# A decoder layer on one core: first queries sent in two parts, and splits of weights, x, context, tables and mask moved to other steps of self-attention

## The chip, the cores and the metric

The kernel runs on one core of a Trainium2 chip. The metric is the time of one execution on the device, in microseconds. The kernel before took 874.06 us, the median of three runs (873.6 to 877.2).

## What is computed

One decoder layer with normalisation after each part, on x of 8 batches of 128 tokens of 512 features, in float32:

```
x = layernorm(x + self_attention(x))         # 32 heads of 16, causal, biases
x = layernorm(x + cross_attention(x, ctx))   # 32 query heads, 8 key/value heads of 128, rotary, mask
x = layernorm(x + ffn(x))                    # 4-bit weights, 512 -> 1376 -> 512, silu gate

def self_attention(x):
    q, k, v = x @ Wq.T + bq, x @ Wk.T + bk, x @ Wv.T + bv      # 32 heads
    att = softmax(where(causal, q @ k.T / 4, -inf))
    return (att @ v) @ Wo.T + bo
```

## The kernel before, in words

Each float32 operand is split into a high half and a low half in float16 and each product is done as three float16 products (`split_products`, lines 353 to 355). "High half" is the rounded operand, "low half" what is left of it.

**Self-attention** is done in 8 blocks of 8 steps, with `t` the number of the step, from -12 to 69. A block `j` is one quarter of the heads (8 of them) for one half of x (4 batches). Step `t` of block `j = t // 8`, with `n = t % 8`, has the scores of one batch and four heads. Blocks 0 to 3 use the first half of x, blocks 4 to 7 the second. Every engine runs its own instructions in the order in which the program writes them, step by step, and waits on semaphores; nothing is reordered by the chip. What an engine does in a step beside its regular work is set by tables of step numbers (`W1_SLOT`, `X_SLOT`, `CTX_SLOT`, `TABLE_SLOT`, `MASK_SLOT` and so on).

The regular work of step `t`:

- TensorE (PE): `scores1(t)` (the causal mask as a matmul, line 1579, then two products of stacked keys and queries, line 1582); in steps 4 and 5 of a block a half each of the keys of block j + 2 (`keys1`), in 6 and 7 of its queries (`queries1`), in 0 to 3 a batch each of the values of block j + 1 (`values1`); `weigh1(t - 3)`, the products with the values (lines 1606 to 1608); `turn1(t - 1)`, four transposes of the probabilities (line 1591).
- VectorE (DVE): `row_max1(t)` (line 1114), `p1_lo(t - 2)`, the low half of the turned probabilities, and in even steps `normalise`.
- ScalarE (ACT): `exps1(t)` (lines 764 and 813), `p1_hi(t - 1)`, the high half of the turned probabilities, and in step 6 of a block the keys of block j + 2 out of PSUM (`k1_out_f32`), in step 0 the queries of block j + 1 (`q1_out_f32`).
- GpSimd (POOL): the halves of keys and queries from block 1 on, and of some weights and context.
- SP: all loads, in one queue, among them `stack_rows(j)`: keys and queries of block j go to memory and come back stacked. Step 8j waits for them (`stack_in`).

Beside this, until now:

- ScalarE writes the low and high first queries to memory when both are there (`keep_first_queries`, line 903) and brings them back in three loads (`bring_first_queries`, line 908).
- The third block's weights (`w1_split_hi(2, .)`, `w1_split_lo(2, .)`) get their high halves on ScalarE in steps 0, 1, 2 and their low halves on VectorE one step later. SP issues their load when all stacked rows of block 0 have landed, and the load of the fourth block's weights when these low halves are done. Behind that load stand the second half of the context (`load_ctx(1)`), the rotary tables and `stack_rows(2)`.
- The second half of x gets its four high halves on ScalarE in steps 10, 12, 14, 15, its low halves on VectorE one step later (`x_split_lo(1, k)`). `keys1(4, 0)` of step 20 waits for all of them, and so does SP before `load_ctx(0)`.
- The second half of the context is split on VectorE in steps 9, 11, 25, 29 (`ctx_split`, two instructions each), the tables of the 4-bit weights in steps 18 to 21 (shift, digits, zeros, scales), the mask in step 23.

The part of SP's queue on which much depends:

```
sp.wait_ge(xT_lo, NHALF * NK)      # all eight low halves of x
load_ctx(0)
stack_rows(3)
```

## Time and profile before

| | |
|---|---|
| median of 3 runs | 874.06 us (873.6 to 877.2) |
| profiled execution | 874.4 us, of it 872.5 span |
| granted TensorE clock, mean | 0.998 |
| self-attention, steps 0 to 63 | from 23.45 us on, to about 200 us |

| engine | busy us | share |
|---|---|---|
| TensorE | 831.5 | 95% |
| VectorE | 708.9 | 81% |
| GpSimd | 606.8 | 70% |
| ScalarE | 529.0 | 61% |

Times in the views are microseconds from the start of the span. "Idle before" an instruction is time in which its engine had nothing to do, and the arrow names what ended it. A load is shown where it is issued, on the queue of its engine (SPq, ACTq); how long it took from issue to landing is in a view of its own. Each step of self-attention can be found by its mask matmul, line 1579: step 0 is the first of them.

### The profile page before, as it was taken

How to read it: one execution, taken by the hardware profiler on the slowest of the kernel's cores; microseconds unless marked ns; L12 is line 12 of the kernel's file. 1: busy time of each engine (PE TensorE's matmuls, PEld its weight loads, DVE VectorE, ACT ScalarE, POOL GpSimd, SP SyncE). 2: the span in 40 equal slices, each digit the busy share in tenths (PEclk: the TensorE clock that was granted, in tenths of full speed). 3: DMA queues.
4: the chain of work that ended last, by engine and by line, in shares of the span. 5: the costliest groups of instructions: out<-in, count | busy, mean ns of one | idle time of the engine just before them, and what ended most of it. 6: DMA issues, size and time to landing. Idle time of an engine off the chain costs nothing.

```text
span 872.5 us, 17343 instructions
## 1 busy us (share of the span) xinstructions
PE 831.5 (95%) x6125; PEld 467.0 (54%) x6125; DVE 708.9 (81%) x1098; ACT 529.0 (61%) x1551; POOL 606.8 (70%) x534
## 2 busy tenths in 40 slices
PE   8799999998899999989999999999999989999997
PEld 4577777555445555545555555555555544333344
DVE  5588898987777887799789689698889765899897
ACT  4788888444566665656766665665566752777400
POOL 1165959896656775777776667668888642887895
PEclk9999999999999999999999999999999999999999
DMA  6764245203135413424314214213433213230011
GB/s 178 233 211 166 75 139 167 61 2 121 26 91 140 106 32 83 109 43 157 75 31 127 61 37 122 61 37 86 133 83 46 48 26 89 86 121 14 1 48 49
DMA packets 120037, 76.75 MB, mean 88 GB/s; under 512 B 72877, under 2 KB 104336, under 8 KB 119952
## 3 DMA queue, kind: packets, MB, share of 16 engines
q1 hardware_dynamic: 117504, 74.86, 31.5%
q8 instruction: 49, 0.80, 0.4%
q10 hardware_dynamic: 2448, 0.79, 0.4%
q14 instruction: 36, 0.29, 0.1%
HBM read 52.50 MB, written 6.36 MB: 67 GB/s over the span
## 4 chain that ended last, share of the span: by engine, by line
PE 42%; POOL 22%; DVE 13%; ACT 10%; issue 9%; DMA 3%; SPq 0%; ACTq 0%; DVEq 0%; POOLq 0%
PE bank L353 12%; PE bank L354 12%; PE bank L355 12%; POOL rot L634 4%; POOL q2l L640 3%; ACT prob L964 2%; DVE total L1322 2%; ACT prob L813 2%; POOL pn L651 2%; POOL prob L644 2%; POOL xqs L583 1%; POOL deq L663 1%; POOL left L667 1%; POOL xql L587 1%; DVE rsin L1193 1%
## 5 line engine op out<-in xcount | busy, mean ns | idle before, releaser
L644 POOL TENSOR_TENSOR prob<-prob,rden 128x512 f32<-128x512 f32 x64 | 67.9, 1061 | 116.2 <-DVE rden L1251 116.2
L634 POOL TENSOR_TENSOR rot<-rcos,rsin 128x512 f32<-128x512 f32 x80 | 107.0, 1337 | 18.6 <-DVE rsin L1193 18.6
L353 PE MATMUL bank<-aTh,xqh 128*128 128x512 f16 x256 | 97.1, 379 | 4.1 <-DVE rsin L1193 2.4
L353 PE MATMUL bank<-xoh,o2h 128*128 128x512 f16 x256 | 97.0, 379 | 0.9 <-DVE o2l L1083 0.8
L354 PE MATMUL bank<-xol,o2h 128*128 128x512 f16 x256 | 97.0, 379 | 0.0
L355 PE MATMUL bank<-xoh,o2l 128*128 128x512 f16 x256 | 97.0, 379 | 0.0
L355 PE MATMUL bank<-aTh,xql 128*128 128x512 f16 x256 | 97.0, 379 | 0.0
L354 PE MATMUL bank<-aTl,xqh 128*128 128x512 f16 x256 | 97.0, 379 | 0.0
L964 ACT ACTIVATE prob<-bank,ebias 128x128 f32<-128x128 f32 x256 | 90.6, 366 | 2.1
L1193 DVE SCALAR_TENSOR_TENSOR rsin<-bank,sinq 64x512 f32<-64x512 f32 x128 | 88.0, 688 | 1.7
L651 POOL TENSOR_TENSOR pn<-prob,pn 128x512 f16<-128x512 f32 x64 | 84.0, 1313 | 7.0 <-ACT pn L976 6.8
L640 POOL TENSOR_TENSOR q2l<-rot,q2h 128x512 f16<-128x512 f32 x64 | 82.2, 1284 | 4.4 <-ACT q2h L858 4.4
L858 ACT CAST q2h<-rot 128x512 f16<-128x512 f32 x64 | 39.6, 618 | 74.5 <-POOL rot L634 74.3
L764 ACT ACTIVATE ebias<-nmax 128x4 f32<-128x4 f32 x128 | 26.9, 210 | 78.7 <-DVE nmax L1246 57.6
L813 ACT ACTIVATE prob<-bank,ebias 128x128 f32<-128x128 f32 x256 | 73.2, 369 | 2.1
L976 ACT CAST pn<-prob 128x512 f16<-128x512 f32 x64 | 39.4, 616 | 56.6 <-POOL prob L644 56.4
L1083 DVE SCALAR_TENSOR_TENSOR o2l<-bank,o2h 128x512 f16<-128x512 f32 x64 | 43.4, 679 | 34.7 <-ACT o2h L764 33.9
L1193 DVE SCALAR_TENSOR_TENSOR rcos<-bank,cosq 128x512 f32<-128x512 f32 x64 | 43.7, 683 | 25.6 <-PE bank L355 25.6
L1083 DVE SCALAR_TENSOR_TENSOR pT<-bank,pT 128x512 f16<-128x512 f32 x64 | 43.8, 684 | 13.3 <-ACT pT L764 13.1
L1265 DVE SCALAR_TENSOR_TENSOR res<-bank,res 128x512 f32<-128x512 f32 x64 | 43.8, 685 | 12.3 <-PE bank L355 12.1
L1114 DVE TENSOR_REDUCE nmax<-bank 128x4 f32<-128x512 f32 x64 | 43.7, 683 | 11.3 <-PE bank L1582 11.2
L964 ACT ACTIVATION_READ_ACCUMULATOR prob<-bank,ebias 128x1 f32 x256 | 51.9, 203 | 0.0
(218 smaller groups left out, 2644.2 us busy)
## 6 DMA issues: line engine op xcount, KB each, us to landing
tst<-tables SPq DMA_DIRECT2D x11, 768.0 KB, 5.3
xqs<-in_xwq SPq DMA_DIRECT2D x8, 1024.0 KB, 7.1
xos<-in_xwo SPq DMA_DIRECT2D x8, 1024.0 KB, 5.6
qst<-in_fq SPq DMA_DIRECT2D x11, 384.0 KB, 3.3
kstk<-stack SPq DMA_DIRECT2D x48, 64.0 KB, 2.2
qstk<-stack SPq DMA_DIRECT2D x21, 128.0 KB, 2.5
xs<-in_ctxT SPq DMA_DIRECT2D x2, 1024.0 KB, 7.4
res<-in_x SPq DMA_DIRECT2D x1, 2048.0 KB, 8.3
```

Source lines behind the costliest of these rows:

```text
L353: pe.matmul(out_ap, ah, bh, start=first, stop=False)
L354: pe.matmul(out_ap, ah, bl, start=False, stop=False)
L355: return pe.matmul(out_ap, al, bh, start=False, stop=last)
L634: nc.gpsimd.tensor_tensor(rot[:, r % 2, :], rcos[:, r % 2, :], rsin[:, r % 2, :], ALU.add).then_inc(rope_rot, 1)
L640: nc.gpsimd.tensor_tensor(lo, rot[:, r % 2, :], hi, ALU.subtract).then_inc(rope_lo, 1)
L644: nc.gpsimd.tensor_tensor(prob[:, v % 2, :].rearrange("p (h k) -> p h k", h=QH), prob[:, v % 2, :].rearrange("p (h k) -> p h k", h=QH), rd ...
L651: nc.gpsimd.tensor_tensor(pn[:, v % 2, 1, :], prob[:, v % 2, :], pn[:, v % 2, 0, :], ALU.subtract).then_inc(c_pn_lo, 1)
L813: last = nc.scalar.activation(prob[:, u % 2, j * S:(j + 1) * S], bank[2 + u % 2][:, j * S:(j + 1) * S], ACT.Exp, bias=ebias[:, u % 2, j:j ...
L964: last = nc.scalar.activation(prob[:, v % 2, j * S:(j + 1) * S], bank[2 + v % 2][:, j * S:(j + 1) * S], ACT.Exp, bias=ebias[:, v % 2, j:j ...
L1083: return nc.vector.scalar_tensor_tensor(out=dst, in0=src, scalar=2.0 ** e, in1=hi, op0=ALU.mult, op1=ALU.subtract)
L1193: last = nc.vector.scalar_tensor_tensor(out=as_batches(dst[to, r % 2, :]), in0=as_batches(bank[f % 2][src, :]), scalar=2.0 ** (e - E_X - E_W),
L1265: nc.vector.scalar_tensor_tensor(out=r, in0=bank[6 + v % 2][:, :], scalar=2.0 ** (-E_V2 - E_W), in1=r, op0=ALU.mult, op1=ALU.add).then_inc ...
```

## The change

```
-X_SLOT = {0: 10, 1: 12, 2: 14, 3: 15}
-CTX_SLOT = {(1, 0): 9, (1, 1): 11, (1, 2): 25, (1, 3): 29}
+X_SLOT = {0: 10, 1: 13, 2: 15, 3: 17}
+X_LO_SLOT = {0: 11, 1: 15, 2: 17, 3: 19}
+CTX_SLOT = {(1, 0): 9, (1, 1): 23, (1, 2): 25, (1, 3): 33}
...
-TABLE_SLOT, MASK_SLOT, BIAS_SLOT, SCALES_SLOT = 18, 23, 17, 26
+TABLE_SLOTS = 26, 27, 30, 31
+MASK_SLOT, BIAS_SLOT, SCALES_SLOT = 34, 17, 26
...
-                sp.wait_ge(q1_out, 32 * (j + 1))
+                sp.wait_ge(q1_out, 32 * j + 16)
...
+            stack_rows(4)
             sp.wait_ge(tab_ready, 2)
             for t, src in enumerate((z1, sw)):
                 sp.dma_start(tables_d[t], src[:, :]).then_inc(tab_out, 16)
-            stack_rows(4)
             stack_rows(5)
...
-                pool.wait_ge(q1_out, 32 * j)
+                pool.wait_ge(q1_out, 32 * j - 16)
+                if j == 1:
+                    pool.wait_ge(q1_first, 16)
...
-            def keep_first_queries():
+            def keep_first_high():
+                act.wait_ge(first_hi, 2)
+                act.dma_start(stack_d[0, 2], q1h[:, :]).then_inc(q1_first, 16)
+
+            def keep_first_low():
                 act.wait_ge(first_lo, 2)
-                for i, src in enumerate((q1h, q1l)):
-                    act.dma_start(stack_d[0, 2 + i], src[:, :]).then_inc(q1_out, 16)
+                act.dma_start(stack_d[0, 3], q1l[:, :]).then_inc(q1_out, 16)

             def bring_first_queries():
-                act.wait_ge(q1_out, 32)
                 for slot, part in enumerate((2, 2, 3)):
+                    if part == 2:
+                        act.wait_ge(q1_first, 16)
+                    else:
+                        act.wait_ge(q1_out, 16)
...
+                if t == FIRST + 4:
+                    keep_first_high()
                 if t == FIRST + 5:
-                    keep_first_queries()
+                    keep_first_low()
...
-                if t in (0, 1, 2):
-                    w1_split_hi(2, t)
+                if t in (2, 3, 4):
+                    w1_split_hi(2, t - 2)
...
-                if t in (1, 2, 3):
-                    w1_split_lo(2, t - 1)
-                for k, slot in X_SLOT.items():
-                    if slot == t - 1:
+                if t in (3, 4, 5):
+                    w1_split_lo(2, t - 3)
+                for k, slot in X_LO_SLOT.items():
+                    if slot == t:
...
-                    if t == TABLE_SLOT + step:
+                    if t == TABLE_SLOTS[step]:
...
+                if t == 0:
+                    values1(1, 0)
                 if 0 <= t < STEPS1:
                     scores1(t)
...
-                if j + 1 < BLOCKS and n < 4:
+                if j + 1 < BLOCKS and n < 4 and t != 0:
                     values1(j + 1, n)
```

The high first queries are written as soon as they are there, the low ones when they are, and the two loads that need only the high ones are issued without waiting for the low ones. The third block's weights are rounded in steps 2, 3, 4 (low halves 3, 4, 5). The high halves of the second half of x go to steps 10, 13, 15, 17, the low ones to 11, 15, 17, 19. Two pieces of context move from step 11 to 23 and from 29 to 33, the tables from 18 to 21 to 26, 27, 30, 31, the mask from 23 to 34, and SP writes the tables behind block 4's rows. On TensorE the first value product of block 1 moves ahead of the first scores.

On TensorE at step 0, before (the scores are the first two rows, lines 1579 and 1582; `[waits ...]` are semaphores):

```order
L1579 MATMUL bank<-tri,identb 128x512 [waits consts_ready,stack_in0]
L1582 MATMUL bank<-kstk,qstk 128x256 x2
L353 MATMUL bank<-w1h,aTh 128x128 [waits k1_f32,w1_lo]
L354 MATMUL bank<-w1l,aTh 128x128
L355 MATMUL bank<-w1h,aTl 128x128
```

and in the change, from the last three of the twelve value matmuls on:

```order
L355 MATMUL bank<-w1h,aTh 128x128
L356 MATMUL bank<-w1l,aTh 128x128
L357 MATMUL bank<-w1h,aTl 128x128
L1591 MATMUL bank<-tri,identb 128x512 [waits consts_ready,stack_in0]
L1594 MATMUL bank<-kstk,qstk 128x256 x2
```

The twelve value matmuls now stand ahead of the wait for the stacked rows (`stack_in0`), not behind it.

On VectorE in steps 18 to 20, before, from the normalising of step 18 on (`znb` are the table digits, `nmax` the row maxima, `pT` the low half of the probabilities):

```order
L1270 TENSOR_TENSOR znb<-tz,shz 33x512 [waits codes_tab_in]
L1114 TENSOR_REDUCE nmax<-bank 128x4 [waits exp_done,s_psum]
L1083 SCALAR_TENSOR_TENSOR pT<-bank,pT 128x512 [waits pv_done,pT_hi]
L1280 TENSOR_SCALAR znb<-znb 33x512 [waits tab_step]
L1114 TENSOR_REDUCE nmax<-bank 128x4 [waits exp_done,s_psum]
```

and in the change:

```order
L1142 TENSOR_TENSOR onrm<-bank,rden 128x128 [waits rden_done]
L1126 TENSOR_REDUCE nmax<-bank 128x4 [waits exp_done,s_psum]
L1095 SCALAR_TENSOR_TENSOR pT<-bank,pT 128x512 [waits pv_done,pT_hi]
L1095 SCALAR_TENSOR_TENSOR aTl<-xs,aTh 128x512 [waits xT_hi]
L1126 TENSOR_REDUCE nmax<-bank 128x4 [waits exp_done,s_psum]
```

The table shift and digits are gone from here, and x's last low half (`aTl`) stands in the place of the digits.

## Rows read from the trace of the kernel before

**Rows 1.** TensorE's waits, 0 to 345 us: total us, times, longest

```profile
PE bank L1591 <- ACT prob L813: 7.8, 8, 2.6
```

**Rows 2.** Timeline, TensorE, opening: start us, us, what [idle before <-releaser]

```profile
23.45 0.39 PE L1579 MATMUL bank<-tri,identb 128*128 128x512 bf16 x1 [1.66 <-DMA qstk<-stack]
...
24.56 0.38 PE L1579 MATMUL bank<-tri,identb 128*128 128x512 bf16 x1
...
30.63 0.66 PE L1591 MATMUL bank<-ident,prob 128*128 128x128 f32 x4 [2.62 <-ACT prob L813]
```

**Rows 3.** Timeline, ScalarE and its queue, opening

```profile
16.36 0.45 ACTq L906 DMA_DIRECT2D stack<-q1l  x1
...
19.43 1.99 ACTq L911 DMA_DIRECT2D qstk<-stack  x3
...
28.68 0.63 ACT L764 ACTIVATE w1h<-w1s 128x512 f16<-128x512 f32 x1 [1.90 <-DMA w1s<-in_wvT]
```

**Rows 4.** DMA issues up to 60 us: KB each, us from issue to landing

```profile
xs<-in_ctxT SPq DMA_DIRECT2D x1, 1024.0 KB, 9.1
...
stack<-q1l ACTq DMA_DIRECT2D x1, 128.0 KB, 3.1
```

**Rows 5.** Timeline, TensorE: steps 8, 19, 24, 32, 40, 48 and two stalls

```profile
43.92 0.38 PE L1579 MATMUL bank<-tri,identb 128*128 128x512 bf16 x1
...
57.97 0.17 PE L1606 MATMUL bank<-v1h,pT 128*128 128x17 f16 x1 [1.44 <-DVE onrm L1130]
...
71.19 0.38 PE L1579 MATMUL bank<-tri,identb 128*128 128x512 bf16 x1
...
83.87 0.38 PE L1579 MATMUL bank<-tri,identb 128*128 128x512 bf16 x1
...
103.41 0.38 PE L1579 MATMUL bank<-tri,identb 128*128 128x512 bf16 x1
...
122.12 0.38 PE L1579 MATMUL bank<-tri,identb 128*128 128x512 bf16 x1
...
129.81 0.17 PE L1606 MATMUL bank<-v1h,pT 128*128 128x17 f16 x1 [0.54 <-DVE onrm L1130]
...
140.88 0.38 PE L1579 MATMUL bank<-tri,identb 128*128 128x512 bf16 x1
```

**Rows 6.** Timeline, SP's queue: third block's weights, and context behind the fourth's

```profile
23.41 0.40 SPq L392 DMA_DIRECT2D w1s<-in_wkT  x1
...
36.91 0.52 SPq L479 DMA_DIRECT2D xs<-in_ctxT  x1
```

**Rows 7.** Timeline, VectorE: context (step 11), x's last low half, shift, digits

```profile
53.19 1.38 DVE L1093 TENSOR_SCALAR cTh<-xs 128x512 f16<-128x512 f32 x1
54.61 0.98 DVE L1083 SCALAR_TENSOR_TENSOR cTl<-xs,cTh 128x512 f16<-128x512 f32 x1
...
67.50 0.68 DVE L1083 SCALAR_TENSOR_TENSOR aTl<-xs,aTh 128x512 f16<-128x512 f32 x1
...
72.11 0.85 DVE L1270 TENSOR_TENSOR znb<-tz,shz 33x512 int32<-33x512 int32 x1
...
74.08 1.51 DVE L1280 TENSOR_SCALAR znb<-znb 33x512 int32<-33x512 int32 x1
```

**Rows 8.** Timeline, SP's queue: context, and the query loads of block 3

```profile
68.21 0.38 SPq L479 DMA_DIRECT2D xs<-in_ctxT  x1
...
77.40 1.37 SPq L425 DMA_DIRECT2D qstk<-stack  x3
```

**Rows 9.** DMA issues, 78.3 to 78.6 us: the last of those three

```profile
qstk<-stack SPq DMA_DIRECT2D x1, 128.0 KB, 4.0
```

**Rows 10.** Stretches: us, busy of PE, PEld, DVE, ACT, POOL, clock, DMA, GB/s

```profile
28.00:30.00 2.00, 0.01 (x1) 0.00 (x0) 0.66 (x2) 1.29 (x5) 0.69 (x1) 1.00 0.47 158
...
238.00:240.00 2.00, 2.00 (x16) 1.90 (x15) 1.75 (x4) 1.51 (x3) 2.00 (x3) 0.50 0.02 4
```

**Rows 11.** Timeline, TensorE, the stall ahead of the lower clock

```profile
236.97 0.91 PE L1658 MATMUL bank<-ident,res 128*128 128x128 f32 x4 [2.98 <-DVE rsin L1193]
```

More of the change, by code:

```diff
@@ L318, in decoder_kernel @@
         qk_hi, qk_lo = sem("qk_hi"), sem("qk_lo")
-        k1_out, q1_out, stack_in = sem("k1_out"), sem("q1_out"), [sem("stack_in0"), sem("stack_in1")]
+        k1_out, q1_out, q1_first, stack_in = sem("k1_out"), sem("q1_out"), sem("q1_first"), [sem("stack_in0"), sem("stack_in1")]
         s_psum, nmax_done, ebias_done, exp_done = sem("s_psum"), sem("nmax_done"), sem("ebias_done"), sem("exp_done")
```

## Prediction, before the changed kernel was run

> **What bounds the kernel now.** I read the page first: TensorE is busy for 95% of the span, so there are some 40 us in all to be won, and only where TensorE waits. The whole change lies in the first 48 steps of self-attention. The list of TensorE's waits up to 345 us comes next; its longest entry is the transposes of the probabilities, 7.8 us in 8 times [rows 1]. The timeline then tells where. At step 0 TensorE stands 1.66 us until the first queries have landed; at step 1 it stands 2.62 us, because ScalarE has not written the second probabilities [rows 2]. ScalarE in its turn was held for 1.90 us by the third block's value weights, still on their way [rows 3]. At 57.97 there is a third stall, 1.44 us, behind VectorE [rows 5]. The rest of the stretch is nearly tight: the eight steps from 122.12 to 140.88 take 18.76 us with one stall of 0.54 in them, so an unhindered block of eight takes about 18.2 [rows 5]. A reader should keep two questions apart: how early a step could start, and whether its stacked keys and queries have landed by then.
>
> **Opening, part by part.** The low first queries are issued at 16.36 and land 3.1 us later [rows 3, 4]; only then are the three loads issued, from 19.43 for 1.99 us [rows 3]. In the change the high ones are written about 1 us earlier, two of the three loads go ahead of the low ones' landing, and the third is issued at some 19.1 instead of 21.0. So the queries land near 21.7, when TensorE ends its work anyway (23.45 less the idle 1.66 is 21.8). The first value product of block 1 now stands ahead of the first scores: 12 matmuls, step 0's 1.11 us less 0.44 for the scores [rows 2], 0.67. Scores of step 0 at 22.5 instead of 23.45.
>
> The third block's weights now leave ScalarE after three exponentials instead of before the second. The load is issued at 23.41, when the queries have landed [rows 6], and was awaited until 28.68 [rows 3]; issued near 21.9 it is in by 27.2, and ScalarE comes to it at 29.3. The transposes of step 1 follow 2.8 us after step 0's scores and one exponential later, at 27.1 instead of 30.63. Some comes back: the key product of step 4 wants the low half of these weights, which VectorE can end only at 30.9, 0.85 us after TensorE gets there. From step 5 on ScalarE has the same work as before. Step 8, at 43.92 before [rows 5], then starts at 40.6: **-3.3** (between -2.0, if only the DMA wait of 1.9 goes, and -3.8 without the key wait).
>
> **Steps 9 to 14.** What was moved later lets step 9 down: its piece of context stays where it was. The context is issued at 36.91 and lands 9.1 us later, 46.0 [rows 4, 6]. It is queued behind the fourth block's weights, which wait for the third block's last low half, now two steps later. I put its issue at 38.6 and its landing at 46.0 again, since less is in flight ahead of it. VectorE gets there at 44.7 and stands 1.4 us; step 12 has won only 1.9. At step 11 the second piece of context goes away, 1.38 and 0.98 us [rows 7], and with it the stall of 1.44. Step 14 began right behind those products, at 58.7, and now starts at 55.3: **-3.4** (between -2.5 and -5.0 without the wait for the context).
>
> **The step on which it turns: 19.** x's last low half moves from 67.50 [rows 7] in step 16 to the place where the digits now stand, 74.08 [rows 7]. The table shift of 0.85 ahead of it is gone and ScalarE has one high half less before it; in the time base of before it ends at 73.5. Less the 3.4 won that is 70.1, where it was 68.2. Two engines wait for it. TensorE's key product of step 20 needs it: 1.0 us of idle. And SP: the load of the first half of the context waits for all of x and sits **ahead of block 3's stacked rows** on the same queue. In the trace the context is issued at 68.21, right behind x's last half; the last three query loads of block 3 start at 77.40 for 1.37 us and the last of them, at 78.35, needs 4.0 us [rows 8, 9]. That is 14.2 us from x to stacked queries, and nothing of the 14.2 is changed. Before they lay there at 82.35 and step 24 began at 83.87 [rows 5]: 1.5 us of slack. Now they are there at 70.1 + 14.2 = 84.3, while TensorE would be ready at about 80.0. It stands 4.3 us at step 24, and all that was won before is gone: **+0.4** at step 24 (between -1.2 and +1.3, from the bounds of step 14).
>
> **Blocks 3 and 4** (83.87 to 103.41 to 122.12 [rows 5]; 19.54 and 18.71 us, 1.3 and 0.5 above 18.2). Block 3 loses the context piece of step 29 and gains shift and digits, 0.85 and 1.51 us [rows 7], behind the piece of step 25; walking VectorE, ScalarE and TensorE through the eight steps I get 19.1, **-0.4**. Block 4 takes the piece at step 33 and the mask at step 34, of about 0.7 us; TensorE stands some 0.6 at step 35, where before it stood 0.4 at step 32: **+0.2** (each within 1 us). The fifth block's rows no longer wait behind the tables; they had a slack of many microseconds. The tables now wait for step 31, ahead of block 5's rows, which GpSimd ends only after step 30's keys: nothing. The mask and the tables are wanted from step 62 on: nothing, covered by 20 steps and more. GpSimd's new wait for the high queries is long met. The piece of context in step 23 lies under the stall of step 24; if that cover is gone it costs what it cost at step 11, up to 1.4.
>
> **Sum:** 874.4 (the profiled execution, span 872.5 and 1.9 around it) + 0.4 - 0.4 + 0.2 = 874.6; the median of the runs is 0.3 lower, so **874.2**. From the bounds its own range is 872.4 to 876.4.
>
> **The clock.** Around 28 to 30 TensorE did next to nothing for 2 us, in a stall of 2.62, and the granted clock stayed at 1.00. Before 236.97 it did nothing for 2.98 us, and from 238 to 240 the granted clock is 0.50, the lower of the two levels, 1.2 GHz [rows 2, 10, 11]. A stall of 4.3 us at step 24 is longer than either. Two to three and a half microseconds of tight work at half the clock would cost 1.0 to 1.7 us. The Trainium skill (TensorE: Matmul & The Clock Gate, section "The HAM clock gate") says that the gate cuts the clock to half after TensorE has been idle and gives it back only after it has been busy for a while. By that rule this change, which gathers several small stalls into one long one, is worse than its idle time tells; the trace agrees at 238 and does not at 28.
>
> **Rivals.**
> 1. *No stall at step 24.* If the loads of block 3 get through faster than 14.2 us (the last load alone took 4.0, where first queries took 3.1 [rows 4, 9]), or x is finished earlier, the 3.4 us of step 14 and about 0.6 of block 2 stay: 874.2 - 3.4 - 0.6 - 0.2 = 870.0. Against it: it needs the whole 4.3 us, and the order on SP's queue is the same in both kernels. Half of it gives 872.
> 2. *The clock falls at step 24*, by the paragraph above: 874.2 + 1.2 = 875.4.
> 3. *Slower: VectorE falls behind in steps 25 to 27.* Piece, shift and digits in three steps running are at their longest 1.38 + 0.98 + 0.85 + 1.51 = 4.7 us on top of 1.4 a step, against 2.0 us a step of TensorE. It is 3.0 late then, less the 0.9 that the chain allows; I had 0.9 in the sum. It decides if GpSimd's work runs beside all four, since I take these lengths for its doing (a low half of the same shape takes 0.68 or 0.98 [rows 7]). Once in block 3 and once, with the mask, in block 4: 874.2 + 1.2 + 1.0 = 876.4, more where the context also lands late.
> 4. *The change doesn't do what it says in the opening*: ScalarE's write of the high queries lands no earlier, since it shares the way with six key loads. Step 0 is then unchanged and the later steps still win 2; since step 24 hangs on the other end, the total is hardly touched: 874.6.
>
> **How the numbers follow.** What a measurement of this kernel can tell from no change is about 0.5%, 4.4 us. The forecast (rival 4 in it) has 0.50, rival 1 or half of it 0.22, rival 2 0.18, rival 3 0.10. Below 869.7 lies about half of rival 1 with the wait for the context also gone, 0.13; above 878.4 only rivals 2 and 3 together with a late context, 0.05; between them 0.82. The range leaves out a tenth at either end: 869.6 to 877.0.
>
> **What would show it.** In the profile after: the first scores near 22.5 and no wait of ScalarE for weights; a wait of VectorE for the context before step 9's piece; x's last low half near 70; SP issuing the context right behind it and the queries of block 3 some 9 to 10 us later; TensorE idle for 3 to 5 us before the scores of step 24, put down to the stacked queries; and step 40 near 122 as before. If step 24 starts before 82 without such an idle, the argument on SP's queue is wrong and the kernel is faster; if the granted clock shows 0.50 near 84, rival 2 is at work.

## The result, and the profile after

The changed kernel takes **878.45 us** (median of 8 runs, 874.4 to 880.37) where the kernel before takes 874.34 beside it (8 runs, 873.59 to 877.2). The ratio is 1.0037, 95% interval 1.0026 to 1.0049. Measured a second time, it took 880.04 beside 874.38, ratio 1.0055 (1.0041 to 1.0069). So the change makes the kernel slower, by about half a per cent; the forecast was 874.2 with a range up to 877.0, and the measured time lies 1.4 us above that range. The profiled execution took 878.48 us, of it 876.6 span, 4.1 more than the span of before.

The list of TensorE's waits up to 345 us; the columns are who waited for whom, then us in total, times, longest:

```profile
PE bank L1603 <- ACT prob L817: 4.8, 4, 1.6
PE bank L1618 <- DVE onrm L1142: 4.0, 4, 2.0
PE bank L1591 <- DMA qstk<-stack: 3.6, 2, 3.0
```

The longest entry of before, the wait for the probabilities, has fallen from 7.8 us in 8 times [rows 1] to 4.8 in 4. In its place stand a wait for VectorE's normalised product of 2.0 us and one for stacked queries of 3.0. The timeline of TensorE in the change says where (mask matmuls, L1591, mark the starts of steps 0, 8, 12, 14, 24, 32, 40, 48 and 63):

```profile
22.66 0.39 PE L1591 MATMUL bank<-tri,identb 128*128 128x512 bf16 x1 [0.56 <-DMA qstk<-stack]
...
25.46 0.66 PE L1603 MATMUL bank<-ident,prob 128*128 128x128 f32 x4 [1.08 <-ACT prob L817]
...
30.88 0.39 PE L355 MATMUL bank<-aTh,w1h 128*128 128x512 f16 x1 [0.59 <-DVE w1l L1095]
...
40.60 0.38 PE L1591 MATMUL bank<-tri,identb 128*128 128x512 bf16 x1
...
49.75 0.17 PE L1618 MATMUL bank<-v1h,pT 128*128 128x17 f16 x1 [2.00 <-DVE onrm L1142]
...
50.80 0.63 PE L1591 MATMUL bank<-tri,identb 128*128 128x512 bf16 x1
...
57.34 0.38 PE L1591 MATMUL bank<-tri,identb 128*128 128x512 bf16 x1
...
71.83 0.38 PE L355 MATMUL bank<-aTh,w1h 128*128 128x512 f16 x1 [0.86 <-issue]
...
84.81 0.61 PE L1591 MATMUL bank<-tri,identb 128*128 128x512 bf16 x1 [3.00 <-DMA qstk<-stack]
...
104.98 0.38 PE L1591 MATMUL bank<-tri,identb 128*128 128x512 bf16 x1
...
124.28 0.38 PE L1591 MATMUL bank<-tri,identb 128*128 128x512 bf16 x1
...
143.42 0.38 PE L1591 MATMUL bank<-tri,identb 128*128 128x512 bf16 x1
...
197.41 0.38 PE L1591 MATMUL bank<-tri,identb 128*128 128x512 bf16 x1
...
248.01 0.43 PE L355 MATMUL bank<-aTh,xqh 128*128 128x512 f16 x1 [2.13 <-DVE aTl L1095]
```

The rows of before that answer to 57.34, 197.41 and 248.01 and were not shown yet (timeline of TensorE, kernel before: steps 14 and 63, and the same product of cross-attention):

```profile
58.74 0.38 PE L1579 MATMUL bank<-tri,identb 128*128 128x512 bf16 x1
...
194.89 0.38 PE L1579 MATMUL bank<-tri,identb 128*128 128x512 bf16 x1
...
245.51 0.38 PE L353 MATMUL bank<-aTh,xqh 128*128 128x512 f16 x1 [0.78 <-DVE aTl L1083]
```

From these rows and [rows 5], after less before, and what the prediction said of each:

| | before | after | difference | forecast |
|---|---|---|---|---|
| step 8 | 43.92 | 40.60 | -3.32 | -3.3 |
| step 14 | 58.74 | 57.34 | -1.40 | -3.4 |
| step 24 | 83.87 | 84.81 | +0.94 | +0.4 |
| step 32 | 103.41 | 104.98 | +1.57 | 0.0 |
| step 40 | 122.12 | 124.28 | +2.16 | +0.2 |
| step 48 | 140.88 | 143.42 | +2.54 | +0.2 |
| step 63 | 194.89 | 197.41 | +2.52 | +0.2 |
| end of the span | 872.5 | 876.6 | +4.1 | +0.2 |

The gain of the opening is there to two hundredths of a microsecond. It is lost in three places: between steps 8 and 14, at step 24 with what follows it, and once more between 197 and 252 us, in a part of the kernel that the change does not touch. Another 1.0 us goes between steps 32 and 48, in two smaller pieces. The clock shows at each of the first three. Stretches of the change, with the columns of [rows 10] (the third number from the right is the granted clock):

```profile
50.00:52.00 2.00, 2.00 (x16) 1.32 (x13) 1.60 (x4) 1.97 (x7) 1.85 (x3) 0.56 0.58 176
52.00:54.00 2.00, 2.00 (x9) 0.75 (x8) 1.32 (x3) 1.97 (x7) 2.00 (x2) 0.59 0.52 142
...
84.00:86.00 2.00, 1.19 (x7) 0.79 (x8) 0.11 (x1) 0.00 (x0) 1.31 (x2) 0.59 0.77 180
86.00:88.00 2.00, 2.00 (x28) 2.00 (x27) 1.66 (x4) 1.35 (x5) 0.00 (x0) 0.56 1.03 392
...
248.00:250.00 2.00, 1.99 (x6) 0.78 (x7) 1.66 (x3) 0.87 (x5) 0.77 (x1) 0.55 0.01 1
250.00:252.00 2.00, 2.00 (x7) 0.74 (x6) 0.00 (x0) 1.97 (x9) 0.00 (x0) 0.60 1.01 165
```

Behind each of the stalls of 2.00, 3.00 and 2.13 us TensorE runs for about four microseconds at a mean clock of 0.55 to 0.60, that is mostly at 1.2 GHz. The mask matmul of 0.63 at 50.80, where it takes 0.38 elsewhere, is the same thing seen in one instruction.

What released the first two stalls is on VectorE and on SP's queue. VectorE's timeline of the change, step 9's piece of context, step 10's normalised product and x's last low half:

```profile
46.42 0.53 DVE L1105 TENSOR_SCALAR cTh<-xs 128x512 f16<-128x512 f32 x1 [1.86 <-DMA xs<-in_ctxT]
...
49.31 0.29 DVE L1142 TENSOR_TENSOR onrm<-bank,rden 128x128 f32<-128x128 f32 x1
...
70.94 0.78 DVE L1095 SCALAR_TENSOR_TENSOR aTl<-xs,aTh 128x512 f16<-128x512 f32 x1
```

SP's queue in the change, the two loads of context and the query loads of block 3:

```profile
38.51 0.51 SPq L481 DMA_DIRECT2D xs<-in_ctxT  x1
...
71.75 0.38 SPq L481 DMA_DIRECT2D xs<-in_ctxT  x1
...
81.34 1.37 SPq L427 DMA_DIRECT2D qstk<-stack  x3
```

VectorE stands 1.86 us for the context at step 9. SP issues the next context when x's last low half ends at 71.7 (70.94 + 0.78). Behind it on the same queue stand the writes of block 3's keys and queries to memory (issued from 72.26 on) and the loads that bring them back stacked (from 78.13 on); the query loads come 9.6 us after x, and TensorE starts step 24 at 84.81, 13.1 us after x: the chain of the prediction, link by link.

### The profile page after: what moved, and what is told of

It is laid out like the page before. It is cut to its first block, busy times and chain, and to the rows that moved or that the text cites. A ratio compares the mean times of both kernels' runs of the same rounds, so it can differ in the third digit from the quotient of the medians.

```text
span 876.6 us, 17343 instructions
## 1 busy us (share of the span) xinstructions
PE 834.1 (95%) x6125; PEld 467.6 (53%) x6125; DVE 710.2 (81%) x1098; ACT 530.2 (60%) x1551; POOL 607.5 (69%) x534
## 4 chain that ended last, share of the span: by engine, by line
PE 43%; POOL 23%; DVE 12%; issue 9%; ACT 8%; DMA 4%; SPq 1%; DVEq 0%; POOLq 0%; ACTq 0%
PE bank L355 12%; PE bank L356 12%; PE bank L357 12%; POOL rot L638 4%; POOL q2l L644 3%; POOL pn L655 2%; DVE total L1334 2%; ACT prob L976 2%; POOL prob L648 2%; POOL left L671 1%; POOL xqs L587 1%; POOL deq L667 1%; ACT prob L817 1%; POOL xql L591 1%; DVE rsin L1205 1%
## 5 line engine op out<-in xcount | busy, mean ns | idle before, releaser
L988 ACT CAST pn<-prob 128x512 f16<-128x512 f32 x64 | 39.4, 615 | 57.2 <-POOL prob L648 56.9
```

## Experiments

Each kernel was timed in five rounds beside the kernel before on the same chip. That took 874.92 us beside x_early, opening, ctx_behind and busy, 874.85 beside x_alone and the three with the first piece of context late (these four ran on another chip than the rest), 874.89 beside x_alone_behind, all_three and busy_q, and 874.38 beside the last. All edits are to the changed kernel unless it says otherwise, and each kernel has a label, by which the expectations and tables name it.

### x back in its early steps (x_early), and the opening alone (opening)

```
-X_SLOT = {0: 10, 1: 13, 2: 15, 3: 17}
-X_LO_SLOT = {0: 11, 1: 15, 2: 17, 3: 19}
+X_SLOT = {0: 10, 1: 12, 2: 14, 3: 15}
+X_LO_SLOT = {0: 11, 1: 13, 2: 15, 3: 16}
```

> The changed kernel with the second half of x split in the steps of before (high halves 10, 12, 14, 15, low halves one step later); all the rest as changed. Theory A (queue): x's last low half ends near 64, SP issues the context and block 3's rows then, and they have landed by about 78, so TensorE has no stall before step 24 and no half clock behind it. Step 24 starts near 81 and the kernel takes 872 to 873, 1 to 2 us below before. Theory B (VectorE is overfull in blocks 3 and 4 through tables, context and mask): step 24 moves but the blocks behind it stay long, and the kernel stays at 876 or above. The stall of 2 us in step 11 and the half clock behind it are there under both.

**871.95 us** (870.88 to 874.37), ratio 0.9966 (0.995 to 0.9982). No stall at step 24, which begins at 82.07, 1.1 us later than theory A had it.

The second kernel has that edit too, and context, tables, mask and SP's order as in the kernel before, so that only the opening is changed:

```
-CTX_SLOT = {(1, 0): 9, (1, 1): 23, (1, 2): 25, (1, 3): 33}
-TABLE_SLOTS = 26, 27, 30, 31
-MASK_SLOT, BIAS_SLOT, SCALES_SLOT = 34, 17, 26
+CTX_SLOT = {(1, 0): 9, (1, 1): 11, (1, 2): 25, (1, 3): 29}
+TABLE_SLOTS = 18, 19, 20, 21
+MASK_SLOT, BIAS_SLOT, SCALES_SLOT = 23, 17, 26
```

> Only the opening of the change: first queries written apart, first value product ahead of the first scores, third block's weights two steps later; x, context, tables and mask in the steps of before, SP's order as before. Theory A: step 8 starts near 40.6 (3.3 us earlier); VectorE then waits 1.9 us for the context in step 9 and has the second piece in step 11, so a part is given back; no stall before step 24. Kernel 871.5 to 873.5. If the opening itself were harmful, because what follows waits for loads in any case, it would take 874 or more.

**872.72 us** (871.75 to 874.67), ratio 0.9976 (0.9965 to 0.9986). The opening alone is worth 2.2 us, and moving the second piece of context, the tables and the mask costs nothing in sum (871.95 with them, 872.72 without, and the intervals overlap). The loss of the change comes in with the slots of x.

### The slots of x alone in the kernel before (x_alone), and with SP's queue turned round (x_alone_behind)

The kernel before with the slots of x of the change:

```
-X_SLOT = {0: 10, 1: 12, 2: 14, 3: 15}
+X_SLOT = {0: 10, 1: 13, 2: 15, 3: 17}
+X_LO_SLOT = {0: 11, 1: 15, 2: 17, 3: 19}
...
-                    if slot == t - 1:
+                    if slot == t:
```

> The kernel before with one edit: the high halves of the second half of x in steps 10, 13, 15, 17 and the low ones in 11, 15, 17, 19, everything else (opening, context, tables, mask, queue order) as before. Theory A (x's last low half holds the context's load, which holds block 3's stacked rows): step 20 lies near 73, x's last low half ends near 74.5, and the queries of block 3 land 13.1 us later as in the change, at 87.6; TensorE stands about 3 us or more ahead of the scores of step 24, which begin at 87 to 88 instead of 83.87; with the clock halved behind that stall 878 to 880.5. Rival B (the slots of x cost nothing themselves, the change loses by VectorE's and ScalarE's new pieces in later steps): step 24 within 1 us of 83.9, 874 to 875.5.

**879.65 us** (877.45 to 881.5), ratio 1.005 (1.0036 to 1.0063). TensorE at step 24 and SP's queue ahead of it:

```profile
88.44 0.61 PE L1580 MATMUL bank<-tri,identb 128*128 128x512 bf16 x1 [2.31 <-DMA qstk<-stack]
```

```profile
74.53 0.38 SPq L480 DMA_DIRECT2D xs<-in_ctxT  x1
...
85.03 1.39 SPq L426 DMA_DIRECT2D qstk<-stack  x3
```

The context is issued at 74.53, right behind x's last low half; the query loads at 85.03; step 24 starts at 88.44 instead of 83.87. Then the same kernel with two entries of SP's queue turned round:

```
-            sp.wait_ge(xT_lo, NHALF * NK)
-            load_ctx(0)
             stack_rows(3)
+            sp.wait_ge(xT_lo, NHALF * NK)
+            load_ctx(0)
```

> The kernel before with the x slots of the change, as in x_alone (879.65 us, step 24 at 88.44), and the queue turned round: SP loads block 3's stacked rows ahead of the first half of the context. Theory A (the loss of x_alone goes through SP's queue): no stall behind the stacked queries, step 24 at 84.5 to 85.5, only the key product of step 20 waits 1.4 us for x's last low half; no half clock near 84 to 88; 875 to 876.5. Rival B (the x slots cost VectorE or TensorE time by themselves): step 24 at 87 or later, 878 or more.

**874.61 us** (873.33 to 877.03), ratio 1.0002 (0.9991 to 1.0013), 0.4 below the range of theory A. SP's queue and step 24 now:

```profile
73.95 1.37 SPq L426 DMA_DIRECT2D qstk<-stack  x3
75.37 0.43 SPq L480 DMA_DIRECT2D xs<-in_ctxT  x1
```

```profile
84.92 0.38 PE L1580 MATMUL bank<-tri,identb 128*128 128x512 bf16 x1
```

x's last low half ends at 73.47, in x_alone at 74.50 (all of this difference stood already at step 8, 43.24 for 44.27). The query loads come 11 us earlier, there is no wait for them, and 5.0 us of the kernel's time are back. This pair shows the cause: the slots of x cost through the wait for x that stands ahead of block 3's stacked rows. With the queue turned, step 24 still begins 1.05 us later than in the kernel before (TensorE's wait of 1.44 us for x at the key product of step 20, with the half clock behind it), but block 3 takes 18.34 us instead of 19.54, and in sum nothing is left. Whether the turn of the queue alone would make the kernel before faster was not run.

### The same turn of the queue in the change (ctx_behind)

> The changed kernel with one thing turned round on SP's queue: block 3's stacked rows first, then the wait for all of x and the first half of the context. x stays late. Theory A: the key product of step 20 still waits 0.9 us for x, but the stall of 3.0 us before step 24 and the half clock behind it go: step 24 near 82, kernel 872.5 to 874. If instead the late x itself (VectorE, step 20) were the cause, step 24 would stay near 84 to 85 and the kernel at 877 to 878.

**873.74 us** (871.62 to 874.92), ratio 0.9984 (0.9973 to 0.9994), 4.7 below the change, as theory A had it. Step 24 starts without a wait, 1 us earlier than expected:

```profile
81.01 0.38 PE L1591 MATMUL bank<-tri,identb 128*128 128x512 bf16 x1
```

### TensorE kept busy in the two stalls (busy), by matmuls whose results nobody reads

```
+                if t == 24:
+                    pe.wait_ge(exp_done, 23)
+                    for _ in range(12):
+                        pe_.matmul(bank[2][:, :]..., identb[:, :], tri[:, :]..., start=True, stop=True)
...
+                if t == 11:
+                    pe.wait_ge(q1_f32, 3)
+                    for _ in range(8):
+                        pe_.matmul(bank[1][:, :]..., identb[:, :], tri[:, :]..., start=True, stop=True)
```

> The changed kernel with matmuls that compute nothing wanted put into two stalls of TensorE: 8 in step 11 (1.7 us of the 2.0) and 12 before step 24 (2.6 us of the 3.0), into banks that are free there. The waits stay; only the idle time is filled. Clock theory: the granted clock stays at 1.00 around 50 to 54 and 84 to 88, the work behind each stall takes its full-clock time, 1.5 us less behind step 11 and 1.3 us less behind step 24: kernel 875.5 to 876.5. Rival (the half clock costs nothing because other engines bound those steps anyway): 878 to 878.5, as changed.

**875.43 us** (874.44 to 880.01), ratio 1.001 (0.9996 to 1.0024): twenty matmuls more, and the kernel is 3.0 us faster than the change. The stretches behind the two stalls:

```profile
50.00:52.00 2.00, 1.44 (x21) 1.19 (x21) 1.67 (x6) 1.97 (x8) 1.85 (x3) 1.00 0.28 87
52.00:54.00 2.00, 2.00 (x24) 1.34 (x22) 1.28 (x3) 2.00 (x7) 2.00 (x2) 1.00 0.48 141
84.00:86.00 2.00, 1.53 (x21) 1.07 (x20) 0.57 (x1) 0.00 (x0) 1.24 (x2) 1.00 0.80 201
86.00:88.00 2.00, 2.00 (x38) 1.84 (x36) 1.70 (x5) 1.81 (x7) 0.00 (x0) 1.00 1.02 376
```

What released the stalls comes no earlier (step 24 begins at 84.79, in the change at 84.81), but the clock behind them is 1.00. Steps 8 to 14 take 15.59 us (41.20 to 56.79) instead of 16.74, and steps 24 to 32 take 18.90 (84.79 to 103.69) instead of 20.17: the half clock cost 1.15 and 1.27 us where it fell. (Counted from the end of the wait at step 11 to step 14, the change takes 7.59 us and busy 6.16. The change profiled again, below, takes 6.16 as well: its clock stayed at 1.00 there with no matmul added. So the half clock itself costs 1.43 at the first place; in busy 0.28 of it is lost again because the wait ends that much later after step 8.) The first of the two does not reach step 24, which hangs on the queries. The second does reach the end, less what another half clock near 164 us takes back: step 63 begins 1.15 earlier than in the change (196.26). The other 1.35 of the 2.5 between the two profiled spans (874.1 and 876.6) lie behind step 63, of which more below.

### The first piece of context in a later step (ctx0_late), with the turned queue, with the early x, and with both

```
-CTX_SLOT = {(1, 0): 9, (1, 1): 23, (1, 2): 25, (1, 3): 33}
+CTX_SLOT = {(1, 0): 21, (1, 1): 23, (1, 2): 25, (1, 3): 33}
```

> The change with one edit: the first piece of context is split in step 21 instead of 9, so that VectorE waits for no load at step 9; x and the queue order as in the change. Theory A: VectorE's wait of 1.9 us at step 9, TensorE's stall of 2.0 at step 11 and the half clock behind it go; step 14 begins at 54.5 to 55.5 instead of 57.34, and x's last low half ends near 69 to 70; step 24 still stands behind the stacked queries, 13.1 us after x, at 82.5 to 83.5 instead of 84.81, with a stall of 3 us or more and the half clock behind it. So 876 to 877.5: about two thirds of what is won at step 14 comes through. Rival B (step 24 is not bound by x): the whole gain of 2 to 3 us at step 14 and no stall at 24, 872 to 874.

**874.03 us** (872.83 to 876.59), ratio 0.9993 (0.9984 to 1.0001). Step 14 begins at 53.95 and step 24 at 82.12, behind a stall of 3.35 us, both a little earlier than theory A had them. The median fell by 4.4 us, more than A's 1 to 2.5, and lies at the edge of rival B's 872 to 874, so the time does not decide between them. The profile does: the stall at step 24 is there, as only A has it, but A priced the piece too low. The profiled execution took 875.54, 2.9 less than that of the change, and 2.7 of it is there at step 24. From step 8 to step 14 this kernel takes 12.90 us (41.05 to 53.95) and the change 16.74; the 3.84 between them are TensorE's stall of 2.00 and 1.84 of half clock and what follows from it. This is the step where the prediction's 3.4 went.

With SP's queue turned round as well (ctx0_late_behind):

> The change with two edits: the first piece of context is split in step 21 instead of 9, and SP loads block 3's stacked rows ahead of the first half of the context. Theory A: neither the stall at step 11 nor the one at step 24 is left, step 14 near 55, step 24 at 79.5 to 80.5, and no half clock up to 230 us; what is left is block 3's own work. 870.5 to 873. Rival B (VectorE, which now has context pieces in steps 21, 23 and 25 and the shift and digits in 26 and 27, is the next to bind): step 24 as said, but step 32 more than 19.8 us later than it, 873 to 875.

**869.52 us** (869.1 to 869.86), ratio 0.9936 (0.9924 to 0.9948), the lowest median of all, though the intervals of the next two kernels overlap with it. It is 1 us below the range of theory A. Step 24 starts at

```profile
77.97 0.38 PE L1591 MATMUL bank<-tri,identb 128*128 128x512 bf16 x1
```

without a wait, 5.9 us before that of the kernel before and 1.5 earlier than expected, and the granted clock is 1.00 up to 230 us. Step 32 follows at 97.73, 19.76 behind; rival B's bound of 19.8 was not passed.

With x in its early steps instead of the turned queue (ctx0_late_x_early):

> The change with two edits: the first piece of context is split in step 21 instead of 9, and the halves of x are back in steps 10, 12, 14, 15 and 11, 13, 15, 16. Theory A: the opening's 3.3 us come through to step 14 (near 55.5) and to step 24 (80 to 81), since x's last low half ends at 65 to 66 and the queries land before 80. With x_early at 871.95 and its stall of 2.69 at step 12 with the half clock behind it gone, 869.5 to 871.5. Rival B (something later takes the gain back): within 0.5 of x_early.

**870.01 us** (869.88 to 870.15), ratio 0.9942 (0.9929 to 0.9955). The time is in the range of theory A; step 14 at 53.08 and step 24 at 77.59 both lie 2.4 us earlier than it had them. And with all three edits (all_three):

> The change with three edits: first piece of context in step 21, block 3's stacked rows ahead of the context on SP's queue, x back in steps 10, 12, 14, 15. Theory A: of ctx0_late_behind (869.52) the key product's wait of 1.26 us at step 20 goes, step 24 begins at 77.0 to 77.6, 868.5 to 869.5. Rival B: blocks 3 and 4 are bound by VectorE behind it, and step 32 stays at 97.7: within 0.3 of 869.7.

**869.74 us** (869.2 to 871.73), ratio 0.9947 (0.9934 to 0.996). The time is rival B's: the key product no longer waits and step 24 comes 0.31 earlier (77.66), but step 32 lies at 97.86, no earlier than with two edits. That VectorE binds block 3 there is not shown: TensorE waits for it 0.6 us in the block, in the kernel with two edits as well. Either way of freeing the queries is enough, and they do not add.

### The rest of the loss, behind 197 us

In the change the last 1.6 us are lost where nothing was changed. The stall of 2.98 us is at 236.97 before [rows 11] and at 239.50 after. Before, the clock fell behind it (0.50 from 238 to 240, [rows 10]) and the next stall, at 245.51, was 0.78. After, it stayed at 1.00, the next stall, at 248.01, was 2.13, and the clock fell there. From the one stall to the other both took the same (8.54 and 8.51 us): VectorE sets that time, TensorE only waits more or works more slowly. Behind the second stall TensorE no longer waits for VectorE, and there the half clock costs its full price: the nine products from 248.01 on take 3.62 us, those from 245.51 on 1.94. From the mask matmul of step 63 to the end of the span:

| half clock behind the | kernel: us |
|---|---|
| first stall | before 677.6, x_early 677.1, opening 677.3, busy 677.8, x_alone_behind 677.2, ctx0_late_behind 677.7, ctx0_late_x_early 678.1, all_three 678.1 |
| first, twice as long | x_alone 678.2 |
| second stall | change 679.2, change again 678.7, ctx_behind 679.3, ctx0_late 678.9 |

(The labels are those of the expectations above; "before" and "change" are the two kernels.) These sums still mix the place of the half clock with what comes later. A fixed instruction shortly behind the second stall parts the two; it is VectorE's fifth reciprocal of cross-attention, here before and in the change:

```profile
250.42 0.18 DVE L1251 RECIPROCAL rden<-dens 128x4 f32<-128x4 f32 x1
```

```profile
254.61 0.18 DVE L1263 RECIPROCAL rden<-dens 128x4 f32<-128x4 f32 x1
```

It comes 55.5 us after the mask matmul of step 63 before, and 57.2 in the change, so the whole 1.6 us is lost by then. In the nine kernels whose half clock falls behind the first stall it comes after 55.5 to 55.9 us, in the four profiles of the last row after 57.2 each time: the place costs 1.3 to 1.7 us. From there to the end all fourteen profiles (busy_q, below, included) take 621.5 to 622.5 us. The four highest of these, x_alone, ctx0_late_x_early, all_three and busy_q, are those with one more stretch of half clock between 388 and 404 us.

One kernel was to test this, busy_q, with eight more matmuls, read by nobody, in the second stall of the change:

```
+                    if what == (2, 0):
+                        for _ in range(8):
+                            pe_.matmul(dst[:, :]..., identb[:, :], tri[:, :]..., start=True, stop=True)
                     pe.wait_ge(fill_free, find_fill("t", 0, BH * ORDER[n][1] + BH - 1) + 1)
```

> The change with eight matmuls more, 1.7 us of TensorE work whose result nobody reads, in the stall of 2.13 us ahead of the query product of the third block of cross-attention (248.01 in the change). Everything up to 245 us as in the change. Theory A (the last 1.65 us of the loss is the clock at half behind this stall, in the place where it was not in the profile before): the granted clock is 1.00 from 248 to 252, the nine products of 0.43 us take 0.22, and the kernel takes 876.5 to 877.3. Rival B (the loss there is the waits of VectorE and not the clock): 878 to 878.9, clock 1.00 all the same. If the half clock falls behind the earlier stall of 2.98 this time, where before it cost nothing, the median is 876.8 as well and the profile must tell the cases apart.

**878.49 us** (877.3 to 878.93), ratio 1.0041 (1.0029 to 1.0053). It told nothing of that (from step 63 on it took 678.7, and 56.3 to the fixed instruction): the clock fell behind the first stall this time, TensorE came to the second one late, and the eight matmuls of 1.89 us then stood in the way of the query product (249.31, where 8.54 us after the first stall's end would be 248.52). The last run was the change itself once more (after_again, "change again" in the table):

> The changed kernel itself, profiled a second time, to see which parts of its loss belong to the kernel and which to one execution. Expected of both executions: VectorE's wait for the context of 1.9 us and TensorE's stall of about 2.0 to 2.4 at step 11, the stall of 2.7 to 3.4 us at step 24 with the clock at half behind it, step 48 at 143 to 144. Theory A (whether the half clock falls behind the stall of 2.98 us near 239, where it costs nothing, or behind the next one near 248, is decided in each execution): this time it may fall at 240, and then the time from the last mask matmul of self-attention to the end is 677.1 to 678.2 us instead of 679.2. Theory B (it belongs to the kernel): at 248 again, 679.2. In both the median is 877.5 to 879.

**880.04 us** (877.23 to 880.39), ratio 1.0055 (1.0041 to 1.0069). TensorE's timeline at step 11, at step 24 and in cross-attention:

```profile
50.79 0.17 PE L1618 MATMUL bank<-v1h,pT 128*128 128x17 f16 x1 [2.71 <-DVE onrm L1142]
...
86.22 0.39 PE L1591 MATMUL bank<-tri,identb 128*128 128x512 bf16 x1 [4.33 <-DMA qstk<-stack]
...
250.39 0.48 PE L355 MATMUL bank<-aTh,xqh 128*128 128x512 f16 x1 [2.13 <-DVE aTl L1095]
```

Several things expected of both executions did not come: the stalls are longer (2.71 and 4.33 us), the clock stays at 1.00 behind the one at step 11, step 48 begins at 145.87, and the median is 1.0 above the range. TensorE also stands 1.34 us for VectorE at step 27, where the profile of the change shows 0.46: the piece of context in step 25 took VectorE 2.83 us instead of 1.95. The half clock lies behind the second stall again (theory B's place), but the time from step 63 on is 678.7 and not 679.2. Whether the place belongs to the kernel or to the execution is not settled by two profiles. No kernel moved it on purpose either, so that the place costs 1.3 to 1.7 us is read from thirteen profiles and not from an experiment.

## Why the prediction was wrong

**What held.** *Opening*: step 8 at 40.6, measured 40.60; first scores 22.66 for 22.5, the key product's wait 0.59 for 0.85. *The step on which it turns*: TensorE stands at step 24 behind the stacked queries, because x's last low half holds the context's load; x_alone and x_alone_behind show this with one edit between them, 5.0 us apart, and the change and ctx_behind with 4.7. The chain was 13.1 us in one execution and 14.4 in the other (71.81 to 86.22), for a forecast of 14.2. *Opening doing nothing* (rival 4), *no stall* (rival 1): excluded. *Rival 3*, VectorE behind in steps 25 to 27: not what made it slower, since x_early, with all these pieces where the change has them, is 2.97 us faster than the kernel before. It is not absent: in the second profile of the change TensorE waits 1.34 us for VectorE at step 27.

**What failed.** The measured median is 4.25 us above the forecast. By the table of steps, 0.5 of it stands at step 24, 1.0 in block 3, 0.4 in block 4, 0.4 in block 5, and 1.6 behind step 63; the rest, 0.3, is the step from the profiled execution to the median, which this time were the same. What carried the time out of the range is the half clock, which the sum has at nothing: 1.27 us in block 3 and 1.6 behind step 63 (points 3 and 5).

1. *"I put its issue at 38.6 and its landing at 46.0 ... step 12 has won only 1.9"*, and step 14 at 55.3. Issue and landing were right (38.51; VectorE goes on at 46.42), VectorE's wait nearly so (1.86 for 1.4). What was not carried through is that wait's way to TensorE: VectorE, held for 1.86 us and then busy with the piece, ended the normalised product at 49.6, and TensorE stood 2.00 us for it at step 11, in the place of the 1.44 at 57.97 that the change took away [rows 5]. The half clock behind it cost 1.43 more (1.15 in the sum of steps 8 to 14). The term of -3.4 was -1.4; without the wait at step 9 (ctx0_late) step 14 lies at 53.95, -4.8.
2. *"x's last low half ... that is 70.1"*: it was 71.7. The chain behind it was 1.1 shorter in this execution than the 14.2 of the sum, so the term of step 24, +0.4, measured +0.94: near only because two errors met. How much of step 14 gets through to step 24 the run of ctx0_late shows the other way: step 14 3.4 earlier, step 24 2.7.
3. *The clock stood outside the sum*, as rival 2 with a chance of 0.18 and a price of 1.2, since [rows 2, 10] show a stall of 2.62 us with the clock at 1.00 behind it. The price was right (1.27); the chance was not: in both executions of the change, in x_alone, ctx0_late and busy_q, that is in every profile with that stall left idle, the clock fell behind it. The 1.00 of [rows 10] was the case of one execution: in x_alone, whose code is the same up to there, the same stall took 2.60 us and the clock was 0.57 from 30 to 32. This is block 3, forecast at -0.4 and measured at +0.63.
4. *Block 4, +0.2, and block 5, nothing*: +0.59 and +0.38. For block 4 the forecast was right in eight of the ten profiles of kernels with the moved context, tables and mask: 18.90 or 18.91 us, where the four without (before, opening, x_alone, x_alone_behind) have 18.70 to 18.72. The profile of the change and that of ctx0_late have 19.30, because VectorE took 2.35 us for the piece of context in step 33 and not 1.95. The piece in the change and in x_early:

```profile
108.85 1.37 DVE L1105 TENSOR_SCALAR cTh<-xs 128x512 f16<-128x512 f32 x1
110.26 0.98 DVE L1095 SCALAR_TENSOR_TENSOR cTl<-xs,cTh 128x512 f16<-128x512 f32 x1
```

```profile
105.09 0.42 DVE L1105 TENSOR_SCALAR cTh<-xs 128x512 f16<-128x512 f32 x1
105.54 1.53 DVE L1095 SCALAR_TENSOR_TENSOR cTl<-xs,cTh 128x512 f16<-128x512 f32 x1
```

   Block 5 takes 19.12 to 19.14 in all ten and 18.73 to 18.76 in the four: the +0.38 belongs to those moves (or to SP's new order, which came with them), and which of them it is stays open.
5. *Nothing behind step 48*: +1.6, all of it lost within 57 us of step 63, and in place with where the half clock fell near 240 and 248. It could not be read from the diff, but the range could have allowed for it, since [rows 10, 11] show the half clock there.

**The range.** It went up to 877.0, which holds one of the rivals' costs at a time. Here the half clock of block 3 (1.27), which rival 2 had, met with that of cross-attention (1.6), which no term and no rival had, and with 0.8 more than forecast in blocks 4 and 5.

## What to carry to other kernels

A wait at the head of an in-order load queue holds back every load behind it: before a producer is moved later, look for what waits for it on a queue and not only on an engine, and turn the queue's entries round first; here that alone was worth 4.5 to 5.0 us three times. A gain ahead of such a point comes through only by as much as the awaited work itself comes earlier, which is why such edits must be judged together: the change with two small corrections is 0.6% faster than the kernel before, and without them 0.5% slower. A TensorE stall as long as those seen here (the half clock fell behind stalls from 1.4 us up) should be priced with what the half clock behind it may cost, here 1.3 to 1.7 us each in tight work, and the range should take in every such stall, the present ones too.

## What the runs showed of the hardware

**The same stall lowers the clock in one execution and not in the next.** At step 11, in nearly the same code, the clock behind stalls of 2.00 (change), 2.35 (opening) and 2.69 us (x_early) fell to half, as it did behind 2.42 us in busy_q, and behind 2.65 (ctx_behind) and 2.71 us (change again) it stayed at 1.00. TensorE's stall and the stretches behind it, in x_early:

```profile
50.81 0.17 PE L1618 MATMUL bank<-v1h,pT 128*128 128x17 f16 x1 [2.69 <-DVE onrm L1142]
```

```profile
52.00:54.00 2.00, 2.00 (x7) 0.78 (x6) 1.45 (x3) 1.97 (x8) 2.00 (x2) 0.50 0.59 169
54.00:56.00 2.00, 2.00 (x21) 1.33 (x20) 1.65 (x4) 1.62 (x7) 1.85 (x3) 0.72 0.91 176
```

and in the change profiled again, behind 2.71 us at 50.79:

```profile
50.00:52.00 2.00, 1.21 (x19) 1.09 (x20) 1.67 (x5) 2.00 (x7) 1.91 (x3) 1.00 0.49 141
52.00:54.00 2.00, 2.00 (x24) 1.28 (x22) 1.43 (x3) 1.97 (x8) 1.85 (x3) 1.00 0.64 189
```

The length of such a stall does not say whether the clock falls; the shortest of these six lowered it, and so did a stall of 1.44 us at the key product of step 20 in x_alone_behind, whose stretch behind it is this (the one of 1.44 us at 57.97 in the kernel before did not):

```profile
74.00:76.00 2.00, 2.00 (x6) 0.69 (x5) 2.00 (x3) 1.12 (x4) 2.00 (x3) 0.50 0.58 181
```

The Trainium skill (TensorE: Matmul & The Clock Gate, section "The HAM clock gate") says that the activity is looked at over stretches that run on by themselves, so that the moment of a change depends on where in one the work falls; these six stalls agree with that, and no run here set the phase on purpose.

**One low stretch is not always as long as another.** Behind the stalls shown above the clock is low in two or three stretches of 2 us. In x_alone it was 0.50 all the way from 242 to 248 us, and in busy_q from 84 to 90, where TensorE was busy all the time.

**The way of the stacked rows to memory and back is not always as long.** From x's last low half to step 24, with the same order on the queue, it was 12.8, 13.1, 13.1, 13.4, 13.9 and 14.4 us in six profiles (busy_q, change, busy, ctx0_late, x_alone, change again). The change's runs spread over 6.0 us (874.4 to 880.37), those of ctx0_late_behind, where nothing hangs on that chain, over 0.8.
